# One table of propagation rows, separate tiles, Newton roots on VectorE and the edge copies on ScalarE

## The chip, the cores and the metric

The kernel runs on one core of a Trainium2 chip. The metric is the device time of one execution in microseconds (us). A core has five engines that run side by side, each with its own queue of instructions in order: TensorE (PE; its weight loads are shown as PEld), VectorE (DVE), ScalarE (ACT), GpSimd (POOL) and SyncE (SP). They wait for one another through semaphores. Transfers run on 16 DMA engines; here SyncE issues the plain ones and GpSimd the gathers and scatters by row index.

## The reference

Four graph layers on 50000 nodes with 96 features each and 50000 edges sorted by target:

```python
h = relu(layernorm(x)); x = x + L0(h)    # attention over the edges, 8 heads of 12
h = relu(layernorm(x)); x = x + L1(h)    # message network, segment sum, then
    # update = gelu([h, agg] @ uW1 + ub1) @ uW2 + ub2
    # L1 = layernorm(h + update) * ln_g + ln_b
h = relu(layernorm(x)); x = x + L2(h)    # 16 rounds: h = 0.9 * sum(norm * h[row]) + 0.1 * x, with self loops
h = relu(layernorm(x)); x = x + L3(h)    # graph convolution by edge weight, with W and b
# layernorm(x) = (x - mean) / sqrt(var + 1e-5), without gain and bias
```

L0 needs the edge projection E = edge_attr_96 @ We + be for each edge.

## The kernel before

All tables have 96 columns of f32. 128 partitions hold 392 rows each (ROWS = 50176), and work goes in 49 batches (NB) of 8 columns (J), that is 1024 rows a batch. A node that no edge points to has a static row, whose values depend on itself alone; the rows that edges point to live in SLOTS = 128 x 400 further rows. `row_e` holds for each edge the row to gather: below ROWS it is a static one, above it a slot.

The stages follow one another, with a barrier between: graph tables; the projections of all nodes; **the first dense pass** (lines 722 to 949); the attention pass over the edges; the message pass over the edges (the second edge pass); the first propagation round with the dense work of the last layer beside it; 14 middle rounds; the last round; the last convolution.

The first dense pass does two independent things for each batch. For the edges: TensorE turns the edge features (`turn`, L824), ScalarE copies them to SBUF (`turned`, L869), TensorE multiplies by We (`edge_product`, L841), VectorE copies the result out of PSUM (`evict`, L904), SyncE stores it. For the nodes: the update of L1 as if no message came in. TensorE makes the hidden layer (`hidden`, L832), ScalarE its gelu (L876), TensorE the outer layer (L851), VectorE adds h (`add`, L913), takes mean and variance (`stats`: L331, L336), ScalarE the square root (`ln_root`, L341), VectorE the reciprocal and -mean times it (`scale`: L346, L347), ScalarE normalises (`norm`, 8 activations, L354), VectorE multiplies by the gain, adds the bias and the old x (`update`: L931, L932, L936). Then the same again for the layer norm of x2: `stats2`, a root, `scale2`, and `norm2` with relu. The results x2 and y are the two halves of one tile `yx`. SyncE stores x2 once and y twice, into each of the two tables of propagation rows (`y_t[0]`, `y_t[1]`), since the rounds read one and write the other. GpSimd meanwhile scatters the segment pointers into `kv_t`, 8 scatters a batch (L806). Square root and gelu need different tables of ScalarE, and a load (ACT_TABLE_LOAD) stands before the first use of either after the other. The names in the profile leave digits out: `d_` is the tiles of the dense passes.

Each engine's order is written out by hand as a list of (lag, step) pairs given to `skewed`: in tick t the engine does each step in the order of the list, for batch t - lag. Halves of a batch (4 of 8 columns) are g = 0 and 1. In the first dense pass:

```python
skewed(pe, (1, turn(0)), (4, edge_product(1)), (3, outer_layer(0)), (1, turn(1)), (0, hidden(1)),
       (1, hidden(0)), (1, edge_product(0)), (2, outer_layer(1)))
skewed(act, (0, turned(0)), (4, root2), (3, norm), (0, gelu(0)), (-3, slots), (4, norm2), (-1, gelu(1)),
       (2, root), (0, turned(1)))     # root, root2: the two calls of ln_root
skewed(dve, (3, scale), (3, evict(1)), (2, add(0)), (4, scale2), (2, stats), (3, update),
       (0, evict(0)), (1, add(1)), (3, stats2))
```

`Own` lets an engine wait for its own last instruction: `do` issues one and waits for its end before the next. Tiles have four buffers (K = 4, index h) where DMAs are involved, PSUM tiles one for each half.

Of the kernel before, what the change touches and what calls it, by code (L numbers as in the profile page):

```python
# [36 lines left out]
TURN = 8 * P  # L37
assert NB % 2 == 1 and 0 < TAIL < CH
# [6 lines left out]
EPS = 1e-5  # L45

# [104 lines left out]
def program(nc, x, src, dst, edge_attr_32, edge_attr_96, edge_weight,  # L151
# [21 lines left out]
    y_t = [dram(f"y{k}_t", ROWS + SLOTS, D) for k in range(2)]  # L173
# [7 lines left out]
    with outer:  # L181
# [87 lines left out]
        ptr_e = sb("ptr_e", [P, CH])  # L269
# [452 lines left out]
        with ExitStack() as p0:  # L722
# [26 lines left out]
            s_sl, s_one, s_mv, s_sd, s_rn, s_ln, s_x2, s_mv2, s_sd2, s_rn2, s_y0 = map(sem, (  # L749
                "d1_slots", "d1_ones", "d1_stats", "d1_root", "d1_scale", "d1_ln_ready", "d1_x2_ready", "d1_stats2",  # L750
                "d1_root2", "d1_scale2", "d1_y0_ready"))
            s_own1, s_own2, s_own3, s_own4, s_own5 = map(sem, (
                "d1_vector_stats", "d1_vector_scale", "d1_vector_x2", "d1_vector_stats2", "d1_vector_scale2"))

            with nc.Block() as block:
                @block.sync
                def _(sp):
# [28 lines left out]
                    def store(b, n, h):  # L786
                        after(sp, s_y0, b + 1)
                        sp.sem_inc(s_turn_s)
                        sp.dma_start(rows_of(x2n_t, 0, b), yx[:, h, :, D:2 * D]).then_inc(s_st[h], 16)
                        for t in y_t:  # L790
                            sp.dma_start(rows_of(t, 0, b), yx[:, h, :, 0:D]).then_inc(s_st[h], 16)
                    skewed(sp, (6, store_e), (2, load_x), (-2, load), (7, store), (0, load_h0), (-2, load_turned))
                    clear_stale(sp)
                    for h in range(K):
                        sp.wait_ge(s_se[h], 16 * OF[h])
                        sp.wait_ge(s_st[h], 48 * OF[h])
# [62 lines left out]
                def _(act):  # L859
# [32 lines left out]

                @block.vector
                def _(dve):
                    own1, own2, own3, own4, own5 = (Own(dve, s_own1, 1), Own(dve, s_own2, 1), Own(dve, s_own3, 2),
                                                    Own(dve, s_own4, 1), Own(dve, s_own5, 1))
                    V.memset(eaT[D:D + 1], 1.0).then_inc(s_one, 1)
                    V.memset(uT[D:D + 1], 1.0).then_inc(s_one, 1)

                    def evict(g):  # L900
                        def run(b, n, h):
                            dve.wait_ge(s_se[h], 16 * n)
                            after(dve, s_eo[g], b + 1)
                            V.tensor_copy(ee[:, h, 4 * g:4 * g + 4, :], eo[g][:]).then_inc(s_ee[g], 1)  # L904
                        return run
# [1505 lines left out]
```

## Time and profile before

| | us |
|---|---|
| median of 3 runs | 11803.59 (11793.79 to 11810.04) |
| the profiled execution, its span | 11805.1 |
| first dense pass, about | 560 to 1190 of the span |
| attention pass | 1190 to 1860 |
| message pass | 1860 to 2590 |
| first round and last dense work | 2590 to 3160 |
| 14 middle rounds | 3160 to 10185 |
| last round | 10185 to 10740 |
| last convolution | 10740 to 11805 |

The profiled execution's own time is its span, from the first instruction to the last. Over it TensorE is busy for 58%, VectorE 54%, ScalarE 36% and GpSimd 72%. In the rows below a time like 814.62 is the start in us from the span's start, and the number behind it the length of the piece; x8 says that 8 instructions are merged into it; [3.97 <-ACT d_eaT L869] says that the engine sat idle for 3.97 us before it, and what ended that. Busy time does not count the waits, so an engine can be at 80% and yet no wait-free path run through it.

### The profile page before, as it was taken

The page shows a single profiled execution, that of the slowest core. Times are in us where ns is not written, and L with a number is a line of the kernel's source. Part 1 is how long each engine was busy: PE and PEld are TensorE (multiplying, and loading weights), DVE is VectorE, ACT ScalarE, POOL GpSimd, SP SyncE. Part 2 cuts the span into 40 slices and gives each one's busy share as a digit, 9 for nine tenths or more (in the row PEclk, how much of TensorE's full clock was granted, in tenths as well). Part 3 has the DMA queues.
Part 4 walks back from the last instruction along what each step waited for, and adds up shares of the span by engine and source line. Part 5 has one row for each costly group of instructions (what it writes and reads, how often), then busy time and mean ns, then how long its engine had stood idle before and what let it go on. Part 6 is the DMA issues. An engine that isn't in the chain of part 4 may idle for free. (4 is left out here: it accounts for less than half of the span.)

```text
span 11805.1 us, 140168 instructions
## 1 busy us (share of the span) xinstructions
PE 6807.1 (58%) x20914; PEld 4246.3 (36%) x20914; DVE 6395.0 (54%) x24157; ACT 4285.7 (36%) x14616; POOL 8514.7 (72%) x8690
## 2 busy tenths in 40 slices
PE   4688677966665665655555555655555555672000
PEld 4566566654433332333333323323333333352000
DVE  6577897889744444444444444444444444575443
ACT  5699666978622222222222222222222222373000
POOL 6675765747677777777777777777777777776777
PEclk7666667977777777778777777777777777896555
DMA  7998885668754444444444444444444444573222
GB/s 250 303 252 242 274 275 172 216 217 284 229 157 126 118 113 116 117 113 119 113 115 117 113 119 113 115 117 113 119 113 117 115 113 118 150 233 125 65 67 55
DMA packets 970285, 1804.49 MB, mean 153 GB/s; under 512 B 412879, under 2 KB 423549, under 8 KB 970062
## 3 DMA queue, kind: packets, MB, share of 16 engines
q1 hardware_dynamic: 687725, 1384.14, 34.7%
q0 software_dynamic: 282336, 418.19, 17.0%
q14 instruction: 184, 1.50, 0.0%
q8 instruction: 40, 0.66, 0.0%
HBM read 1070.12 MB, written 738.89 MB: 153 GB/s over the span
## 5 line engine op out<-in xcount | busy, mean ns | idle before, releaser
L365 POOL DMA_INDIRECT r_g<-y_t,idx_s x5768 | 5535.4, 960 | 1947.2 <-issue 1841.0
L1945 DVE SCALAR_TENSOR_TENSOR F<-r_g,scan_s,F 128x96 f32<-128x96 f32 x5488 | 1769.1, 322 | 3974.2 <-DMA r_g<-y_t,idx_s 3147.3
L2074 ACT ACTIVATE H<-r_pu,kc_e 128x96 f32 (+1 forms) x5474 | 1340.2, 355 | 5536.1 <-PE r_pu L2046 5502.2
L2046 PE MATMUL r_pu<-r_S,ident 128*128 128x384 f32 x2688 | 1734.3, 793 | 2797.4 <-DVE r_S L1947 2797.4
L2046 PEld LDWEIGHTS r_pu<-r_S,ident 128*128 128x128 f32 x2688 | 679.4, 278 | 3546.9 <-DVE r_S L1947 3212.0
L1947 DVE SCALAR_TENSOR_TENSOR r_S<-r_S,scan_s,r_g 128x96 f32<-128x96 f32 x5488 | 1719.0, 313 | 0.5
L2028 PE MATMUL r_pu<-H,ident 128*128 (+2 forms) x2744 | 1530.1, 649 | 91.4 <-DMA r_c<-c_t 85.5
L2029 PE MATMUL r_pu<-r_c,ident 128*128 128x384 f32 (+1 forms) x2744 | 1349.0, 579 | 0.0
L2028 PEld LDWEIGHTS r_pu<-H,ident 128*128 128x128 f32 x2744 | 778.1, 284 | 765.1 <-issue 654.6
L2029 PEld LDWEIGHTS r_pu<-r_c,ident 128*128 128x128 f32 x2744 | 666.8, 243 | 559.9 <-issue 361.4
L2335 PE MATMUL e_pc<-e_S,B 128*128 128x96 f32 x2 | 0.7, 474 | 1042.5 <-DVE e_o L2379 1042.5
L365 POOL DMA_INDIRECT e_kv<-kv_t,idx_s x392 | 422.2, 1077 | 244.2 <-issue 126.0
L806 POOL DMA_INDIRECT kv_t<-seg_s,idx_s x392 | 404.1, 1031 | 189.5 <-issue 114.3
L2324 POOL DMA_INDIRECT out<-e_o,e_out_s x393 | 432.2, 1100 | 119.7 <-issue 119.7
L365 POOL DMA_INDIRECT e_g<-z_t,idx_s x392 | 388.7, 992 | 166.0 <-issue 119.2
L365 POOL DMA_INDIRECT e_x<-h_t,idx_s x392 | 379.4, 968 | 134.5 <-issue 107.5
L365 POOL DMA_INDIRECT l_g<-y_t,idx_s x392 | 378.2, 965 | 130.8 <-issue 117.6
L365 POOL DMA_INDIRECT n_x<-in_x,idx_s x392 | 370.2, 944 | 139.8 <-issue 117.5
L2335 PEld LDWEIGHTS e_pc<-e_S,B 128*128 128x128 f32 x2 | 0.5, 310 | 1042.7 <-DVE e_o L2379 1042.7
L2369 DVE TENSOR_TENSOR e_g<-e_g,scan_s 128x768 f32<-128x768 f32 x49 | 47.9, 977 | 553.8 <-DMA e_g<-z_t,idx_s 553.8
L649 PE MATMUL n_kb<-w_kvq,n_hT 97*128 97x192 f32 x784 | 241.6, 494 | 126.0 <-ACT n_hT L682 67.8
L673 ACT ACTIVATE n_h<-n_x,n_rn 128x96 f32<-128x96 f32 x784 | 286.0, 458 | 0.5 <-DVE n_rn L347 0.5
(329 smaller groups left out, 11912.6 us busy)
## 6 DMA issues: line engine op xcount, KB each, us to landing
r_c<-c_t SPq DMA_DIRECT2D x686, 384.0 KB
y_t<-H SPq DMA_DIRECT2D x672, 384.0 KB
r_g<-y_t,idx_s POOLq DMA_INDIRECT x5880
kv_t<-n_kv SPq DMA_DIRECT2D x49, 776.0 KB, 6.9
y_t<-d_yx SPq DMA_DIRECT2D x98, 384.0 KB
agg_t<-e_S SPq DMA_DIRECT2D x49, 416.0 KB, 4.6
x1s_t<-e_xb SPq DMA_DIRECT2D x50, 384.0 KB, 4.8
h_t<-e_h SPq DMA_DIRECT2D x50, 384.0 KB, 5.2
```

The costliest lines, as they stand in the source:

```text
L365: G.indirect_dma_start(out=to(j), out_offset=None, in_=table, in_offset=bass.IndirectOffsetOnAxis(ap=idx_s[:, h, j:j + 1], axis=0)).then_i ...
L649: last = T.matmul(kb[i][:, j % 2, :], hT[:, h, j // 4, j % 4 * P:(j % 4 + 1) * P], w_kvq[:, 0:2 * D], start=True, stop=True)
L673: last = A.activation(hh[:, h, s, j, :], xs[:, h, s, j, :], ACT.Relu, scale=rn[:, h, 0, c], bias=rn[:, h, 1, c])
L806: G.indirect_dma_start(out=kv_t.rearrange("r (a w) -> (r a) w", w=WP), out_offset=bass.IndirectOffsetOnAxis(ap=idx_s[:, h, j:j + 1], axis= ...
L1945: own.add(V.scalar_tensor_tensor(out=F[:, 0:D], in0=g[:, j, :], scalar=scan_s[:, h, j, 1:2], in1=F[:, 0:D], op0=ALU.mult, op1=ALU.add))
L1947: last = V.scalar_tensor_tensor(out=S[:, h % 2, j, :], in0=before, scalar=scan_s[:, h, j, 0:1], in1=g[:, j, :], op0=ALU.mult, op1=ALU.add)
L2028: T.matmul(to, ident[:], cols(H, b)[:, c, :], start=True, stop=False)
L2029: T.matmul(to, ident[:], cs[:, h, c, :], start=False, stop=False)
L2046: last = T.matmul(pu[h % 2][g][:], ident[:], S[:, h % 2, 4 * g:4 * g + 4, :], start=False, stop=True)
L2074: last = A.activation(v[:, j, :], pu[h % 2][j // 4][:, j % 4, :], ACT.Copy, scale=k[:, j, 0:1])
L2324: G.indirect_dma_start(out=out, out_offset=bass.IndirectOffsetOnAxis(ap=dst_s[:, h, j:j + 1], axis=0), in_=ot[:, h, j, :], in_offset=None, ...
L2369: own.do(V.tensor_tensor(g_[:, h], g_[:, h], scan_s[:, h, :, 2:3].to_broadcast([P, J, D]), ALU.mult))
```

## The change

Part 1, tables and tiles. The two tables of propagation rows become one: slots of one kind of round, the static rows, slots of the other kind. The static rows are stored once. Two lists of rows (`row_y`) take the place of `row_e` for the gathers from it; they are computed in seven VectorE operations at the start of the message pass, into two tiles that are free by then. The tile `yx` becomes two tiles `x2` and `y0`.

Part 2, roots. The first dense pass has no activation with Sqrt any more. VectorE makes 1 / sqrt(var + eps) itself: a start value by a shift and a subtraction on the bits, and three Newton steps, 13 operations with those for eps and -mean times it. One call serves both layer norms, on 128x16 numbers: the first norm of batch b and the second of batch b - 1. It stands where `scale` stood; `scale2` goes. VectorE has one tick more.

Part 3, edge projection. `evict` moves from VectorE to ScalarE: evict(1) stands where root2 was, evict(0) where root was. The lags stay.

```diff
+Y_STATIC = SLOTS
+Y_SLOTS = [SLOTS + ROWS, 0]
+Y_ROWS = [ROWS + 2 * SLOTS, SLOTS + ROWS]
...
-    y_t = [dram(f"y{k}_t", ROWS + SLOTS, D) for k in range(2)]
+    y_t = dram("y_t", ROWS + 2 * SLOTS, D)
...
-        ptr_e = sb("ptr_e", [P, CH])
+        ptr_e = sb("ptr_e", [P, CH], I32)
+        row_y = [ptr_e, src_i]
...
+        def root_reciprocals(own, mv, rn):
+
+            y, nb, v, u = (rn[:, k] for k in range(4))
+            own.do(V.tensor_scalar(v, mv[:, :, :, 1], EPS, None, ALU.add))
+            own.do(V.tensor_scalar(u.bitcast(I32), v.bitcast(I32), 1, None, ALU.logical_shift_right))
+            own.do(V.tensor_scalar(y.bitcast(I32), u.bitcast(I32), -1.0, float(ROOT_START), ALU.mult, ALU.add))
+            for _ in range(3):
+                own.do(V.scalar_tensor_tensor(out=u, in0=y, scalar=-0.5, in1=y, op0=ALU.mult, op1=ALU.mult))
+                own.do(V.tensor_tensor(u, u, v, ALU.mult))
+                own.do(V.scalar_tensor_tensor(out=y, in0=u, scalar=1.5, in1=y, op0=ALU.add, op1=ALU.mult))
+            return V.scalar_tensor_tensor(out=nb, in0=mv[:, :, :, 0], scalar=-1.0, in1=y, op0=ALU.mult, op1=ALU.mult)
...
-            yx = sb("d1_yx", [P, K, J, 2 * D], F32, p0)
+            y0 = sb("d1_y0", [P, K, J, D], F32, p0)
+            x2 = sb("d1_x2", [P, K, J, D], F32, p0)
             st = sb("d1_st", [P, 2, J, 6], F32, p0)
-            mv = sb("d1_mv", [P, K, J, 2], F32, p0)
-            rn = sb("d1_rn", [P, K, 3, J], F32, p0)
-            mv2 = sb("d1_mv2", [P, K, J, 2], F32, p0)
-            rn2 = sb("d1_rn2", [P, K, 3, J], F32, p0)
+            mv = sb("d1_mv", [P, K, 2, J, 2], F32, p0)
+            rn = sb("d1_rn", [P, K, 4, 2, J], F32, p0)
...
-                        sp.dma_start(rows_of(x2n_t, 0, b), yx[:, h, :, D:2 * D]).then_inc(s_st[h], 16)
-                        for t in y_t:
-                            sp.dma_start(rows_of(t, 0, b), yx[:, h, :, 0:D]).then_inc(s_st[h], 16)
+                        sp.dma_start(rows_of(x2n_t, 0, b), x2[:, h]).then_inc(s_st[h], 16)
+                        sp.dma_start(rows_of(y_t, Y_STATIC, b), y0[:, h]).then_inc(s_st[h], 16)
...
+                    def evict(g):
+                        def run(b, n, h):
+                            act.wait_ge(s_se[h], 16 * n)
+                            after(act, s_eo[g], b + 1)
+                            A.copy(ee[:, h, 4 * g:4 * g + 4, :], eo[g][:]).then_inc(s_ee[g], 1)
+                        return run
+
                     def norm(b, n, h):
                         after(act, s_x2, b - 3)
-                        ln_norm(act, b, hs[:, h], ln[:, h], rn[:, h], s_rn, ACT.Identity).then_inc(s_ln, 1)
+                        after(act, s_rn, b + 1)
+                        for j in range(J):
+                            last = A.activation(ln[:, h, j, :], hs[:, h, j, :], ACT.Identity,
+                                                scale=rn[:, h, 0, 0, j:j + 1], bias=rn[:, h, 1, 0, j:j + 1])
+                        last.then_inc(s_ln, 1)
 
                     def norm2(b, n, h):
-                        act.wait_ge(s_st[h], 48 * n)
-                        ln_norm(act, b, yx[:, h, :, D:2 * D], yx[:, h, :, 0:D], rn2[:, h], s_rn2, ACT.Relu
-                                ).then_inc(s_y0, 1)
-                    skewed(act, (0, turned(0)),
-                           (4, lambda b, n, h: ln_root(act, b, mv2[:, h], rn2[:, h], s_mv2, s_sd2)),
-                           (3, norm), (0, gelu(0)), (-3, slots), (4, norm2), (-1, gelu(1)),
-                           (2, lambda b, n, h: ln_root(act, b, mv[:, h], rn[:, h], s_mv, s_sd)), (0, turned(1)))
+                        act.wait_ge(s_st[h], 32 * n)
+                        after(act, s_rn, b + 2)
+                        k = (h + 1) % K
+                        for j in range(J):
+                            last = A.activation(y0[:, h, j, :], x2[:, h, j, :], ACT.Relu,
+                                                scale=rn[:, k, 0, 1, j:j + 1], bias=rn[:, k, 1, 1, j:j + 1])
+                        last.then_inc(s_y0, 1)
+                    skewed(act, (0, turned(0)), (3, evict(1)), (3, norm), (0, gelu(0)), (-3, slots), (4, norm2),
+                           (-1, gelu(1)), (0, evict(0)), (0, turned(1)))
...
-                    own1, own2, own3, own4, own5 = (Own(dve, s_own1, 1), Own(dve, s_own2, 1), Own(dve, s_own3, 2),
-                                                    Own(dve, s_own4, 1), Own(dve, s_own5, 1))
+                    own1, own2, own3, own4 = (Own(dve, s_own1, 1), Own(dve, s_own2, 12), Own(dve, s_own3, 2),
+                                              Own(dve, s_own4, 1))
+                    own2.do(V.memset(mv[:], 1.0))
+                    own2.loop()
...
-                    def evict(g):
-                        def run(b, n, h):
-                            dve.wait_ge(s_se[h], 16 * n)
-                            after(dve, s_eo[g], b + 1)
-                            V.tensor_copy(ee[:, h, 4 * g:4 * g + 4, :], eo[g][:]).then_inc(s_ee[g], 1)
-                        return run
...
-                        ln_stats(dve, own1, b, hs[:, h], st[:, 0], mv[:, h], s_mv)
+                        ln_stats(dve, own1, b, hs[:, h], st[:, 0], mv[:, h, 0], s_mv)
 
                     def scale(b, n, h):
                         after(dve, s_ln, b - 3)
+                        after(dve, s_y0, b - 4)
                         own2.step(b)
-                        ln_scale(dve, own2, b, mv[:, h], rn[:, h], s_sd, s_rn)
+                        if not (isinstance(b, int) and b == NB):
+                            after(dve, s_mv, b + 1)
+                        after(dve, s_mv2, b)
+                        last = root_reciprocals(own2, mv[:, h], rn[:, h])
+                        own2.end()
+                        last.then_inc(s_rn, 1)
 
                     def update(b, n, h):
                         own3.step(b)
@@ -932,21 +961,16 @@
                         own3.do(V.tensor_tensor(ln[:, h], ln[:, h], r_all[:, 1:2, :].to_broadcast([P, J, D]), ALU.add))
                         own3.end()
                         dve.wait_ge(s_x[h], 48 * (n + 1))
-                        dve.wait_ge(s_st[h], 48 * n)
-                        V.tensor_tensor(yx[:, h, :, D:2 * D], xs[:, h], ln[:, h], ALU.add).then_inc(s_x2, 1)
+                        dve.wait_ge(s_st[h], 32 * n)
+                        V.tensor_tensor(x2[:, h], xs[:, h], ln[:, h], ALU.add).then_inc(s_x2, 1)
 
                     def stats2(b, n, h):
                         after(dve, s_x2, b + 1)
-                        after(dve, s_rn2, b - 3)
+                        after(dve, s_rn, b - 2)
                         after(dve, s_mv2, b)
-                        ln_stats(dve, own4, b, yx[:, h, :, D:2 * D], st[:, 1], mv2[:, h], s_mv2)
-
-                    def scale2(b, n, h):
-                        after(dve, s_y0, b - 3)
-                        own5.step(b)
-                        ln_scale(dve, own5, b, mv2[:, h], rn2[:, h], s_sd2, s_rn2)
-                    skewed(dve, (3, scale), (3, evict(1)), (2, add(0)), (4, scale2), (2, stats), (3, update),
-                           (0, evict(0)), (1, add(1)), (3, stats2))
+                        ln_stats(dve, own4, b, x2[:, h], st[:, 1], mv[:, (h + 1) % K, 1], s_mv2)
+                    skewed(dve, (3, scale), (2, edges_only(add(0))), (2, edges_only(stats)), (3, edges_only(update)),
+                           (1, edges_only(add(1))), (3, edges_only(stats2)), total=NX)
...
+                    row_f, at_y = seg[:, :, 0], seg[:, :, 1]
+                    first.do(V.tensor_copy(row_f, row_e[:]))
+                    first.add(V.tensor_scalar(at_y, row_f, float(SLOTS), None, ALU.add))
+                    first.do(V.tensor_scalar(row_f, row_f, float(ROWS), None, ALU.is_lt))
+                    first.add(V.tensor_copy(row_y[0][:], at_y))
+                    first.do(V.tensor_scalar(row_f, row_f, float(SLOTS + ROWS), float(-SLOTS - ROWS), ALU.mult,
+                                             ALU.add))
+                    first.do(V.tensor_tensor(at_y, at_y, row_f, ALU.add))
+                    first.do(V.tensor_copy(row_y[1][:], at_y))
...
-                        gathers(y_t[1], lambda j: g_[:, h, j, :], h, s_g[h])
+                        gathers(y_t[0:Y_ROWS[1], :], lambda j: g_[:, h, j, :], h, s_g[h])
...
-                        to = y_t[1 - odd]
+                        to = Y_SLOTS[1 - odd]
...
-                                gathers(y_t[odd], lambda j: g_[:, h % GB, j, :], h, s_g[h])
+                                gathers(y_t[0:Y_ROWS[odd], :], lambda j: g_[:, h % GB, j, :], h, s_g[h])
...
-                            A.copy(idx_s[:, h, :], cols(row_e, b)).then_inc(s_ix, 1)
+                            A.copy(idx_s[:, h, :], cols(row_y[odd], b)).then_inc(s_ix, 1)
```

## Rows read from the trace of the kernel before

**Rows 1.** Stretch, length, busy PE, PEld, DVE, ACT, POOL, PEclk, DMA share, GB/s

```profile
620.00:1100.00 480.00, 408.53 (x1718) 314.86 (x1717) 367.12 (x1679) 437.52 (x1017) 342.31 (x334) 0.61 0.92 257
...
3160.00:10185.00 7025.00, 4141.72 (x8339) 2147.45 (x8340) 3044.88 (x11029) 1477.46 (x6852) 5230.24 (x5488) 0.78 0.43 118
```

**Rows 2.** Line 932: count, min/median/max ns, first and last start in us

```profile
L932 DVE TENSOR_TENSOR d_ln<-d_ln,r_all x49: 957/958/1007, 598.1 to 1178.3; 128x768 f32<-128x768 f32 x49
```

**Rows 3.** Timeline, 811 to 825 us: ScalarE and TensorE

```profile
811.72 0.67 ACT L876 ACTIVATE d_uT<-d_pu,c_u 96x512 f32<-96x512 f32 x1
...
812.41 1.28 ACT L341 ACT_TABLE_LOAD   x1
...
814.62 1.06 PE L824 MATMUL d_te<-ident,d_ea 128*96 128x128 f32 x4 [3.97 <-ACT d_eaT L869]
...
815.06 2.96 ACT L354 ACTIVATE d_ln<-d_h,d_rn 128x96 f32<-128x96 f32 x8
...
815.47 3.62 PE L832 MATMUL d_pu<-d_hT,w_ua 96*96 96x512 f32 x4
...
819.17 1.28 ACT L876 ACT_TABLE_LOAD   x1 [1.15 <-PE d_pu L832]
...
820.47 0.68 ACT L876 ACTIVATE d_uT<-d_pu,c_u 96x512 f32<-96x512 f32 x1
...
824.12 0.67 ACT L876 ACTIVATE d_uT<-d_pu,c_u 96x512 f32<-96x512 f32 x1
```

**Rows 4.** The same timeline: VectorE

```profile
814.11 0.20 DVE L346 RECIPROCAL d_rn<-d_rn 128x8 f32<-128x8 f32 x1 [2.19 <-ACT d_rn L341]
814.35 0.17 DVE L347 SCALAR_TENSOR_TENSOR d_rn<-d_mv,d_rn 128x8 f32<-128x8 f32 x1
814.43 0.55 DVE L904 COPY d_e<-d_eo 128x384 f32<-128x384 f32 x1
...
815.36 0.20 DVE L346 RECIPROCAL d_rn<-d_rn 128x8 f32<-128x8 f32 x1
...
815.77 1.38 DVE L331 BATCH_NORM_STATS2 d_st<-d_h 128x6 f32<-128x96 f32 x8
...
817.30 0.64 DVE L336 BATCH_NORM_AGGREGATE d_mv<-d_st 128x2 f32<-128x6 f32 x8 [0.16 <-DVE d_st L331]
...
818.05 0.96 DVE L931 TENSOR_TENSOR d_ln<-d_ln,r_all 128x768 f32<-128x768 f32 x1
...
820.91 0.55 DVE L904 COPY d_e<-d_eo 128x384 f32<-128x384 f32 x1
```

**Rows 5.** Groups by line, 1230 to 2590 us: busy us, mean ns, idle before

```profile
L1163 ACT COPY e_u<-e_ub 128x384 f32<-128x384 f32 (+1 forms) x99 | 46.4, 470 | 0.2 <-PE e_ub L1102 0.2
```

**Rows 6.** Lines 346, 347 as rows 2; timeline of VectorE at 18 us

```profile
L346 DVE RECIPROCAL n_rn<-n_rn x49: 252/253/254, 56.7 to 542.7; 128x16 f32<-128x16 f32 x49
...
L347 DVE SCALAR_TENSOR_TENSOR n_rn<-n_mv,n_rn x49: 174/176/245, 57.0 to 543.0; 128x16 f32<-128x16 f32 x49
...
18.09 0.15 DVE L518 SCALAR_TENSOR_TENSOR dg<-seen,carry 128x1 f32<-128x1 f32 x1
```

**Rows 7.** Timeline, 1182 to 1184 us: the last norm of the stage

```profile
1182.90 0.20 DVE L346 RECIPROCAL d_rn<-d_rn 128x8 f32<-128x8 f32 x1 [0.44 <-ACT d_rn L341]
1183.13 0.17 DVE L347 SCALAR_TENSOR_TENSOR d_rn<-d_mv,d_rn 128x8 f32<-128x8 f32 x1
...
1183.40 2.97 ACT L354 ACTIVATE d_yx<-d_yx,d_rn 128x96 f32<-128x96 f32 x8 [0.60 <-DVE d_rn L347]
```

**Rows 8.** Timeline of TensorE, 1121 to 1134 us, at the lower clock

```profile
1121.82 1.06 PE L824 MATMUL d_te<-ident,d_ea 128*96 128x128 f32 x4 [3.96 <-ACT d_eaT L869]
...
1131.96 1.92 PE L851 MATMUL d_po<-w_u,d_uT 97*128 97x96 f32 x8
```

**Rows 9.** Groups by line and shape, 700 to 1060 us: the scatters

```profile
L806 POOL DMA_INDIRECT kv_t<-seg_s,idx_s x248 | 254.5, 1026 | 106.3 <-issue 72.5 <-ACT seg_s L863 33.8
```

**Rows 10.** Timeline of VectorE at the start of the message pass

```profile
1888.10 0.56 DVE L1555 SCALAR_TENSOR_TENSOR e_g<-e_gate,e_po 128x384 f32<-128x384 f32 x1 [21.12 <-ACT e_gate L1505]
```

More of the change, by code:

```diff
@@ L45 @@
 EPS = 1e-5
+ROOT_START = 0x5F3759DF
 class Own:
@@ L748, in program @@
                 "d1_po_full", "d1_h_ready"))
[L749 to L753, printed above, removed]
+            s_sl, s_one, s_mv, s_rn, s_ln, s_x2, s_mv2, s_y0 = map(sem, (
+                "d1_slots", "d1_ones", "d1_stats", "d1_scale", "d1_ln_ready", "d1_x2_ready", "d1_stats2",
+                "d1_y0_ready"))
+            s_own1, s_own2, s_own3, s_own4 = map(sem, (
+                "d1_vector_stats", "d1_vector_scale", "d1_vector_x2", "d1_vector_stats2"))
             with nc.Block() as block:
@@ L795, in _ @@
                         sp.wait_ge(s_se[h], 16 * OF[h])
-                        sp.wait_ge(s_st[h], 48 * OF[h])
+                        sp.wait_ge(s_st[h], 32 * OF[h])
                 @block.gpsimd
@@ L1717, in load @@
                         sp.dma_start(xn[:, h], rows_of(x2n_t, 0, b)).then_inc(s_xn[h], 16)
-                        sp.dma_start(yn[:, h], rows_of(y_t[0], 0, b)).then_inc(s_xn[h], 16)
+                        sp.dma_start(yn[:, h], rows_of(y_t, Y_STATIC, b)).then_inc(s_xn[h], 16)
                     def load_own(b, n, h):
@@ L1722, in load_own @@
                         sp.sem_inc(s_turn_s)
-                        sp.dma_start(yo[:, h], slots_of(y_t[1], ROWS, b)).then_inc(s_yo[h], 16)
+                        sp.dma_start(yo[:, h], slots_of(y_t, Y_SLOTS[1], b)).then_inc(s_yo[h], 16)
                     def store_c(b, n, h):
@@ L1732, in store_y @@
                         sp.sem_inc(s_turn_s)
-                        sp.dma_start(slots_of(y_t[0], ROWS, b), ys[:, h]).then_inc(s_st[h], 16)
+                        sp.dma_start(slots_of(y_t, Y_SLOTS[0], b), ys[:, h]).then_inc(s_st[h], 16)
                     def store_z(b, n, h):
@@ L1752, in _ @@
                     sp.wait_ge(s_zv, 1)
-                    sp.dma_start(first_slots(y_t[0], ROWS), zs[:]).then_inc(s_zo, 16)
+                    sp.dma_start(first_slots(y_t, Y_SLOTS[0]), zs[:]).then_inc(s_zo, 16)
                     sp.wait_ge(s_zo, 32)
@@ L1809, in slots @@
                     def slots(b, n, h):
-                        gather_rows(act, n, h, row_e, b, s_ix, s_g)
+                        gather_rows(act, n, h, row_y[1], b, s_ix, s_g)
                         after(act, s_ss, b - 3)
@@ L1975, in store @@
                                 sp.sem_inc(s_turn_s)
-                                sp.dma_start(slots_of(to, ROWS, b)[:, J - 1, :], cols(H, b)[:, J - 1, :]
+                                sp.dma_start(slots_of(y_t, to, b)[:, J - 1, :], cols(H, b)[:, J - 1, :]
                                              ).then_inc(s_st, 16)
@@ L1980, in store @@
                             sp.sem_inc(s_turn_s)
-                            sp.dma_start(slots_of(to, ROWS, b), cols(H, b)).then_inc(s_st, 16)
+                            sp.dma_start(slots_of(y_t, to, b), cols(H, b)).then_inc(s_st, 16)
                         after(sp, s_up, r * NB)
@@ L1985, in one @@
                         after(sp, s_z, r + 1)
-                        sp.dma_start(first_slots(to, ROWS), zs[:]).then_inc(s_zo, 16)
+                        sp.dma_start(first_slots(y_t, to), zs[:]).then_inc(s_zo, 16)
                     rounds(sp, one)
@@ L2008, in step @@
                                 done = s_g[h] if j < J - 2 else s_end[j - J + 2]
-                                G.indirect_dma_start(out=g_[:, h % GB, j, :], out_offset=None, in_=y_t[odd],
+                                G.indirect_dma_start(out=g_[:, h % GB, j, :], out_offset=None, in_=y_t[0:Y_ROWS[odd], :],
                                                      in_offset=bass.IndirectOffsetOnAxis(ap=idx_s[:, h, j:j + 1], axis=0)
@@ L2143, in load @@
                         after(sp, s_up, b - 3)
-                        sp.dma_start(yo[:, h], slots_of(y_t[0], ROWS, b)).then_inc(s_ld[h], 16)
+                        sp.dma_start(yo[:, h], slots_of(y_t, Y_SLOTS[0], b)).then_inc(s_ld[h], 16)
                         sp.dma_start(cs[:, h], slots_of(c_t, 0, b)).then_inc(s_ld[h], 16)
@@ L2168, in step @@
                         after(pool, s_ss, b - 3)
-                        gathers(y_t[0], lambda j: g_[:, h, j, :], h, s_g[h])
+                        gathers(y_t[0:Y_ROWS[0], :], lambda j: g_[:, h, j, :], h, s_g[h])
                     skewed(pool, (0, step))
@@ L2213, in slots @@
                         s_g.wait(act, h, 16 * J * n)
-                        A.copy(idx_s[:, h, :], cols(row_e, b)).then_inc(s_ix, 1)
+                        A.copy(idx_s[:, h, :], cols(row_y[0], b)).then_inc(s_ix, 1)
                         after(act, s_ss, b - 3)
```

8 lines of the change are left out of this document (4 added, 4 removed).

## The prediction

> **What bounds the kernel now.** I read the table of stretches first. The change alters only one stage's arithmetic, the first dense pass (560 to 1190 us of the span); in it no engine is full: TensorE 409 of 480 us, ScalarE 438, VectorE 367, GpSimd 342, at a granted clock of 0.61 [rows 1]. So a loop of waits sets its pace. 49 batches pass; the second multiply of the residual update starts at 598.1 in the first and at 1178.3 in the last, 12.09 us apart on the mean, 580.2 us in all [rows 2]. In the middle the distance is 12.40: that from gelu(1) at 811.72 to the next at 824.12 [rows 3].
>
> The timeline shows the loop. ScalarE: gelu(1) at 811.72, a table load at 812.41, a root, then the copies of the turned edge features; TensorE, idle until the copy, turns at 814.62 and makes both hidden products from 815.47 on, 3.62 us at the lower level of the clock; ScalarE loads the other table only then, at 819.17, does gelu(0) at 820.47, 8 relu norms, and gelu(1) at 824.12 [rows 3]. Both table loads (1.28 us, 1.30 from start to next start) stand in this loop of 12.40. VectorE is not in it: it waits for ScalarE's root until 814.11, and starts the update at 818.05, when the norms (815.06 + 2.96 = 818.02) end [rows 3, 4].
>
> **The change, part by part.**
>
> *Roots and tables.* Sqrt goes, so gelu's set stays loaded: two loads and a root leave the loop. Its new length: 12.40 - 2 x 1.30 - 0.2 for the root's step, plus one copy of an edge half before turned(1), 0.47 by the copy of this shape in the next stage [rows 5] = 10.1 us. ScalarE's own work was 438 / 480 of 12.4 = 11.3 us a batch [rows 1]; less 2.57 for tables and 0.6 for roots, plus 2 x 0.47, it is 9.1. ScalarE stops being the bound; what is late next is VectorE.
>
> The Trainium skill, "ScalarE: Activation LUTs", section "What ACT_TABLE_LOAD costs", adds a drain of about 1.38 us to each load of 1.28. Here gelu ends at 811.72 + 0.67, the load starts 0.02 later [rows 3], and there is no room for one. By the page the loop would lose 5.3 us and not 2.6; the sum would be the same, as VectorE takes over before either.
>
> *VectorE's work.* It loses both evictions (0.47 each from start to next start: one and an add of the same size stand from 814.43 to 815.36), the separate scale steps (814.11 to 814.43, 815.36 to 815.77) and its waits for roots. It gains one chain of 13 operations on 128x16 elements, each waiting for the one before. Their forms are not in the trace. The nearest row is the multiply of 128x16 in the first stage, 0.176 us; the gap to a dependent operation is 0.04 (814.11 + 0.20 to 814.35) [rows 4, 6]. So 12 x 0.216 + 0.18 = 2.77 us. Bounds: the smallest operation, 0.15 + 0.04 a step, gives 2.43; the reciprocal of 128x16, 0.253 + 0.04 a step, gives 3.77 [rows 6]. I take the multiply, since 10 of the 13 are multiplies of that size and none divides.
>
> *VectorE's pace.* The queue is in order: chain(b), add(0), stats, update(b), add(1), stats2. The update needs ScalarE's norm, which needs the chain just done. Before, the norm had an eviction, an add and another scale step besides stats beside it. Now:
> - chain 2.77;
> - to the norm 0.10 (1183.13 + 0.17 to 1183.40), norm 2.96, back 0.03: 3.09 [rows 3, 7]. Beside it lie add(0) 0.46 and stats 1.53 + 0.64 = 2.63 [rows 4], so VectorE waits about 0.45;
> - update 2.86 (818.05 to 820.91), add 0.46, stats2 1.53 + 0.64 + 0.04 = 2.21 [rows 4].
>
> Sum 11.39 us a batch. The last three batches have no add(0), 10.93. 45 x 11.39 + 3 x 10.93 = 545.3 against 580.2: 34.9 us less. After the last stats2 the chain takes 2.77 where a root, reciprocal and multiply took about 0.9 (1182.90 - 0.44 of waiting, to 1183.13 + 0.17): 1.9 more [rows 7]. Net 33 us.
>
> *Edge copies on ScalarE.* Priced above. Evict(1) stands between turned(0) and the norm, so it could delay the norm; ScalarE has 11.39 - 9.1 = 2.3 us of slack a batch, waits there for the chain, and TensorE made that product earlier in its order. Cost 0; if ScalarE were late by all of it, 0.47 x 48 = 23 us. The store of the edge half comes later in the order by some us than before, with four buffers behind it: nothing waits.
>
> *TensorE.* Nothing added. Its whole pass at the lower level is 1131.96 - 1121.82 = 10.14, plus 1.92 less the overlap of 0.21 seen at 814.62 to 815.47 = 11.85 us [rows 3, 8]. That is over 11.39. A granted clock of 0.61 on the mean says that it stands at the lower level (0.5) for about four fifths of the time; in the rest it gets ahead, and then idles, 3.97 us before 814.62 [rows 1, 3]. At the lower level it would fall behind by 0.46 us a batch. There is room for about 1 us: from the chain's start, add(1) is due at 2.77 + 3.09 + 2.86 = 8.7, and from turn(1) to the end of the product that it needs it takes some 7.7 (all of the pass but a turn and two products: 11.85 less 0.85, 1.66 and 1.66). Two batches fit. I take 0, by the wait of 3.96 us at 1121.82 as at 814.62 [rows 8]; if the clock never rises, 11.85 is the pace.
>
> *GpSimd.* Eight scatters a batch, each 1.026 + 0.30 of issue [rows 9]: 10.6 us. Below 11.39, so hidden; it becomes the floor if VectorE's steps are all short.
>
> *DMA and SyncE.* One of the two stores of the propagation rows goes, of eight transfers of one size. The 16 DMA engines are busy for 0.92 now [rows 1]; 7/8 of it in 11.39 and not 12.4 us is 0.88. Also, the separate tiles are contiguous in a partition where the pair alternated every 96 numbers; I give that nothing. Neither was what a wait ended on. Both SyncE issue steps are shorter; it waits for TensorE anyway. Gain 0, or 0.1 us a batch if landings of x or h0 come late today, which no row shows; lower bound 0.
>
> *New tables of rows.* Seven VectorE operations on 392 columns are added at the start of the second edge pass. VectorE idles 21.12 us there before its first work [rows 10]; at 1 us each they lie within. A memset ahead of the first dense pass lies beside loads. In the other stages the same bytes are moved from other addresses. The propagation rounds, 7025 of the 11805 us, are paced by GpSimd (5230 us busy, 5488 gathers, and issue) [rows 1]. A gather is issued from a list of rows, and its length has no term of which tensor it is. I take 0. From both sides: 0.003 us a gather either way is 16 us.
>
> Sum: 11805.1, the span of the profiled execution, less 33 = 11772. That execution is 1.5 us above the median of 11803.6, so 11771.
>
> **The rivals.**
>
> *TensorE paces (18%).* For: 11.85 over 11.39, and 0.61 is much low time. Against: with less idling it should be high at least as often. 45 x 11.85 + 3 x 10.93 = 566.0, net 12 less: 11792.
>
> *Short steps (12%).* The chain is 2.43: the pace 11.05, 49 us less: 11755. For: some are single-source operations. Against: each waits for the one before. The scatters' 10.6 are the end of this road.
>
> *Slower: the chain is long (9%).* In VectorE's queue, ahead of the norm, it stands wholly in the loop. At 3.77 a chain the pace is 12.39, the stage 593 and the tail 2.9: 16 us more, 11820. From 0.26 us a step (chain 3.44) on, nothing is left of the gain. For: 13 waits on its own semaphore, each with a register operation ahead; integer operations that no row shows. Against: the dependent pair at 814.11 has such a wait, too, and costs 0.04.
>
> *Tables are not rid of (4%).* If identity were not in gelu's set, ScalarE would switch twice a batch, two loads in the loop as today, and save only the root's step and the store: about 11800. The trace shows relu after gelu without a load; identity only after the root. The Trainium skill, "ScalarE: Activation LUTs", section "Table sets: the hidden batching unit", has identity in every set; no row here shows it behind gelu.
>
> *The rounds shift (7%).* Stores and gathers of a round share one tensor and other banks of memory. At 0.003 us longer a gather, 16 us more than forecast, 11787; at 0.008, slower than before, 11815. For: 60% of the time lies there. Against: paced by issue.
>
> **How the numbers follow.** The forecast (50%) is 11771, its own range 11760 to 11784. About 24 us (0.2%) is what a measurement can tell from no change: faster is below 11780. Faster: nearly all of the forecast (47), short steps (12) = 59%. Same: TensorE (18), tables (4), the forecast's rest (3), half of the rounds (3) = 28%. Slower: the long chain (9), the other rounds (4) = 13%. The range, 11748 to 11802, takes in the short chain's 11755 and TensorE's 11792, and leaves out the long chain and the worst rounds.
>
> **What would show it.** Right: one table load in the stage; updates 11.3 to 11.5 us apart; 13 small operations of 2.6 to 2.9 us in all; VectorE waiting 0.3 to 0.6 us for the norm in each batch; ScalarE waiting for the chain and no more for the hidden product; the DMA share below 0.88 in the stage; the rounds the same to 3 us each. Wrong: updates 11.8 or more apart with TensorE busy and low throughout; a chain over 3.4 us; table loads at each norm; GpSimd with no idle time, which would mean a pace of 10.6; or stages other than this one moving by over 10 us.

## The result, and the profile after

The forecast was 11771 us. Measured: 11818.5 us median of 20 runs (11808.6 to 11830.0) against 11802.1 for the kernel before (20 runs, 11789.3 to 11812.6); the ratio is 1.0016, 95% interval 1.0009 to 1.0022. The change makes the kernel slightly slower where I forecast 0.3% faster, and the time lies above my range. Of the experiments below, e5 to e8 and e13 to e16 ran at 14.3 ms, the kernel before beside them too (14328.9 and 14314.4 us), so no time of theirs is laid beside the others; what is used of them is the counts of instructions and packets and the waits on issue.

The profiled execution has a span of 11827.8 us. The rows of after that answer to [rows 1], the first dense pass and the propagation rounds (length, busy PE, PEld, DVE, ACT, POOL, clock, DMA share, GB/s):

```profile
620.00:1100.00 480.00, 419.08 (x1819) 326.74 (x1818) 419.06 (x2053) 366.67 (x992) 373.39 (x349) 0.63 0.79 236
3173.00:10197.00 7024.00, 4131.01 (x8344) 2139.77 (x8344) 3044.83 (x11033) 1479.05 (x6860) 5230.05 (x5488) 0.78 0.43 118
```

In the dense pass ScalarE and VectorE have changed places: 438 to 367 us busy and 367 to 419. The rounds are as before. The multiply of the update, which answers to [rows 2], and the table load with the edge copy (busy us, mean ns, idle before):

```profile
L961 DVE TENSOR_TENSOR d_ln<-d_ln,r_all x49: 957/959/961, 596.5 to 1155.6; 128x768 f32<-128x768 f32 x49
```

```profile
L899 ACT COPY d_e<-d_eo 128x384 f32<-128x384 f32 x98 | 46.2, 472 | 0.0
...
L891 ACT ACT_TABLE_LOAD x1 | 1.3, 1283 | 0.0
```

48 distances in 559.1 us, 11.65 each (12.09 before). Of the table loads one is left. The first issue for the next stage, on SyncE's load of its rows, came at 1193.4 us before and at 1170.1 now: 23.3 us gained.

The gain is given back two stages later. The first issues of each stage, us of the span, read from the tile that each stage loads first:

| first issue of | before | after | stage, after less before |
|---|---|---|---|
| attention pass | 1193.4 | 1170.1 | first dense pass and all ahead −23.3 |
| message pass (ScalarE's first copy of a turned tile) | 1873.7 | 1852.5 | attention pass +2.1 |
| first round | 2602.2 | 2613.4 | **message pass +32.4** |
| 14 middle rounds | 3160.6 | 3172.9 | first round +1.1 |
| last round | 10191.8 | 10202.0 | middle rounds −2.1 |
| last convolution | 10735.9 | 10747.6 | last round +1.5 |
| end | 11805.1 | 11827.8 | last convolution +11.0 |

The message pass computes what it computed before. VectorE's waits there, 1850 to 2600 us of after (what waits, for what: us in total, times, longest):

```profile
DVE e_g L1588 <- ACT e_gate L1529: 34.3, 5, 17.8
DVE e_g L1588 <- issue: 33.1, 7, 4.8
```

The second row is new; no such row stands in the same answer for before. "Issue" is time in which the engine waited for nothing that the profile shows, and L1588, the first operation of the loop over four batches, has it seven times, once behind each of the seven jumps back to the loop's start. The timeline shows the place:

```profile
2184.50 1.02 DVE L1588 SCALAR_TENSOR_TENSOR e_g<-e_gate,e_po 128x384 f32<-128x384 f32 x2 [4.82 <-issue]
```

What comes with it is in the table of DMA queues (packets, MB, share; queue 14 brings instructions). For 1850 to 2600 us before, then after, then for 2178 to 2184 us of after, the time of this one wait:

```profile
q14 instruction: 28, 0.23, 0.1%
```

```profile
q14 instruction: 59, 0.48, 0.2%
```

```profile
q14 instruction: 2, 0.02, 1.2%
```

31 more packets of 8 KB, 4.4 for each of 7 jumps; over the whole run 184 became 219. By the packets' own times two or three of them start within 6 us of each jump back in after, and none in e1 or e4 below. So at every jump VectorE's queue fetches its own loop again, and the first operation waits for it.

### The profile page after: what moved, and what is told of

Its sections match the earlier page's. It is cut to its first block and busy times, and to the rows that moved or that the text cites. A ratio compares the mean times of both kernels' runs of the same rounds, so it can differ in the third digit from the quotient of the medians.

```text
span 11827.8 us, 140857 instructions
## 1 busy us (share of the span) xinstructions
PE 6797.3 (57%) x20914; PEld 4251.9 (36%) x20914; DVE 6437.1 (54%) x24521; ACT 4178.3 (35%) x14523; POOL 8534.7 (72%) x8690
## 3 DMA queue, kind: packets, MB, share of 16 engines
q14 instruction: 219, 1.79, 0.0%
```

## The experiments

**Theory.** Instructions come in blocks of one packet, 8 KB. The queue can keep the message pass's loop, 327 VectorE instructions a pass (counted in the records between two branches, the same in both kernels), only if it lies in few enough blocks. The change put 138 instructions ahead of it: 131 in the first dense pass (311 and not 242 in a pass of its loop, and 62 more in the batches written out around it) and the seven table operations. **Rival.** What the change does in the message pass, its table operations and the new rows, costs the 32 us.

**e1 to e4: only the place is moved.** One-column VectorE fills into a tile of their own, put once ahead of the loop where VectorE has no work (here e1; the number is 30 in e2 and e3 and 100 in e4):

```diff
                     first.do(V.memset(S[:, K - 1, J - 1, :], 0.0))
+                    for i in range(90):
+                        V.memset(pad[:, i:i + 1], 0.0)
```

> The changed kernel with 90 one-column VectorE fills added once, ahead of the loop of the message pass (the second edge pass); they fall into the 21 us in which VectorE has no work there. Theory (position of the loop): the change added 138 VectorE instructions ahead of this loop, and in that position its 327 instructions have to be fetched again in every pass of the loop, one stall of about 4.8 us in each of 7 passes. 90 instructions more move it by less than one block of 128 and out of that position: no idle time of over 2 us with the releaser issue ahead of L1590, the pass shorter by 30 to 33 us, the whole 11785 to 11792 us. Rival 1 (the cost comes from what the change does in this pass: its table operations, or the new rows being read): the stalls stay, 11818 to 11824. Rival 2 (more instructions ahead of the loop, whatever their number, make it later): worse than after by some us.

> The kernel before with 30 such fills at the same place and nothing of the change. Theory (position): 30 instructions move the loop from the last place in a block of 128 in which it fits to one in which it doesn't: 7 stalls of 4.5 to 5 us ahead of the loop's first operation, and 11832 to 11838 us against 11803. Rival (what the change does in this pass): no stall, 11802 to 11806 us.

> The changed kernel with 30 fills and not 90. Theory (position, period of 128): 10 + 30 = 40 instructions beyond the place of the kernel before is still in the part of the block where the loop doesn't fit: the 7 stalls stay, 11815 to 11825 us. If any shift cures it, they are gone.

> The kernel before with 100 fills. Theory (position, period of 128): 100 beyond the place before is a place like that of the changed kernel with 90 fills: no stalls, 11800 to 11810 us, though more instructions stand ahead of the loop than with 30. Rival (the number of instructions ahead counts, and not their place): stalls as with 30 or worse.

Measured: e1 11785.4 us (ratio to before 0.9982, 0.9973 to 0.9991); e2 11849.6 (1.0034, 1.0021 to 1.0048); e3 one run, 11838.3; e4 one run, 11795.6; the kernel before beside them 11809.9. The waits on issue and the instruction packets, 1850 to 2600 us, of e1 (no stall, so only the packets stand here), then of e2 and e3:

```profile
q14 instruction: 26, 0.21, 0.1%
```

```profile
DVE e_g L1558 <- issue: 30.0, 7, 4.4
```

```profile
q14 instruction: 59, 0.48, 0.2%
```

```profile
DVE e_g L1591 <- issue: 25.8, 7, 3.9
```

```profile
q14 instruction: 60, 0.49, 0.2%
```

e4 has 28 packets there and no such stall. 30 idle fills in the kernel *before*, without any of the change, bring the seven stalls and 40 us (25 to 57 by the interval; the stalls' own 30.0 us lie in it); 90 more instructions in the *changed* kernel take them away, and by the ratios (1.0016 and 0.9982) 40 us with them. The rival has fallen. e2 and e3 came out some 14 us above what I expected; their message passes, 749.6 and 745.3 us, are within what the stalls explain, and the rest is in the rounds (7036.3 and 7050.7 us) and the last convolution (below).

**e5: two Newton steps.** The loop `for _ in range(3)` becomes `range(2)`. That leaves out the last refinement of each root, so the roots are less exact; it is a probe of the chain's place, not the same computation.

> The changed kernel with two Newton steps in place of three (rounds 2 of the root are left out), nothing else. Theory 1 (the chain stands wholly in VectorE's loop of the first dense pass): three operations of 0.21 us less in each of 48 distances, 0.63 x 48 = 30 us: the updates 11.0 us apart, the next stage's first issue near 1140. Rival (another engine is close behind, GpSimd's eight scatters at 10.6 to 11.0 a batch, or TensorE): 11.2 to 11.5 apart, 8 to 20 us. Rival 2 (chain off the loop): 11.6 apart. Theory 2 (position of the loop): 54 VectorE instructions fewer stand ahead of the message pass's loop, 44 before its place in the kernel before, inside a stretch where it fits: no stall of over 2 us with the releaser issue, and the message pass near 716 us, as in e1. Both together: 11750 to 11762 us; with the chain but the stalls kept, 11785 to 11795.

**e6, e7, e8:**

> The new table of propagation rows and its seven VectorE operations, with the first dense pass of the kernel before (one store of its rows fewer), and 90 fills ahead of the message pass's loop to hold it where it fits. Theory (rows at other addresses cost nothing, one store fewer gains nothing): the same stages as the kernel before with 100 fills (e4): dense pass to the next stage 1191 to 1193, message pass 714 to 717, rounds 7031 to 7035, 11792 to 11800 us. Rival 1 (the one table makes the rounds' gathers or the last convolution slower: the changed kernel's profile had 1080 us there against 1069): last convolution 1080 or more and 11805 to 11812. Rival 2 (the store gone gains in the dense pass): its end at 1185 or before.

> The changed kernel with the two copies of the edge projection back on VectorE at their old places in its order, and 30 fills ahead of the message pass's loop. Theory (VectorE's queue paces the dense pass): two copies of 0.47 us come into its loop, less the 0.36 us in which it waits for the norm anyway: 0.58 to 0.94 a batch, 28 to 45 us; updates 12.2 to 12.6 apart, next stage near 1200, so that nothing of the change's gain is left; 11813 to 11830 us against the changed kernel without stalls (e1, 11785). Rival (ScalarE or TensorE paces): 11.6 to 11.8 apart, 11785 to 11795.

> The changed kernel with 118 fills: the loop of the message pass stands 128 instructions beyond its place in the kernel before. Theory (blocks of 128): the same place within a block as in the kernel before: no stalls with the releaser issue, 25 instruction packets in the message pass and not 58. Rival (e1 and e4 hit a stretch by chance, no period of 128): stalls of 3 to 5 us may stand there.

The ratios of e5, e6 and e7 to the kernel before beside them were 1.0058, 0.9998 and 0.9990, and e8 is one run; what is used is the packets. e8 has 185 in the whole run (184 before): the place repeats after 128, as expected. e6 and e7 have 184. e5 has 229, and not where I had looked: its message pass has 24, but its *first dense pass* has these, and the waits at that loop's first two operations (600 to 1580 us):

```profile
q14 instruction: 60, 0.49, 0.2%
```

```profile
DVE d_rn L358 <- issue: 50.3, 9, 7.3
...
DVE d_rn L359 <- issue: 29.3, 9, 4.3
```

Stalls at all nine jumps back of a loop that had become shorter; e8 beside it has 0.9 us on issue at L358 and none at L359. This the theory explains only with the count: from the dense loop's start to the message loop's are 1723 instructions in the changed kernel, 13 blocks and 59. Taking all places together (0 is the message loop's place in the kernel before, counted in instructions ahead):

| kernel | place | modulo 128 | refetched |
|---|---|---|---|
| before | 0 | 0 | no |
| after, e12 | 138 | 10 | yes |
| e2 | 30 | 30 | yes |
| e3 | 168 | 40 | yes |
| e5 | 84 | 84 | no |
| e7, e11 | 219 | 91 | no |
| e6, e10 | 97 | 97 | no |
| e4, e13, e17 | 100 | 100 | no |
| e1, e14, e15, e18 | 228 | 100 | no |
| e9, e16 | 114 | 114 | no |
| e8 | 256 | 0 | no |

A loop of 327 touches three blocks of 128 if it starts in the first 58 places of a block, and four otherwise. The column fits if the kernel before stood at one of the places 48 to 57. Then the changed kernel's dense loop stood at one of the first 9 places of a block, and e5's, 15 earlier, across its border: four blocks for 287 instructions. Its second stall fits this too: the border would lie 7 to 15 instructions behind the loop's start, and in the records L359, which waits, is the 11th.

The Trainium skill, "Runtime: NRT & Kernel Launch", section "Instruction fetch mechanics", says that a taken branch whose target is out of the instruction window forces a fetch, an "ifetch stall"; the traces agree. It gives blocks of 256 instructions, two of them held. By that a loop of 327 would be refetched in one stretch of 70 places out of 256; the table has it at 30, 138 and 168 and not at 84 to 114 or 219 to 256, which is no such stretch, and 1.79 MB in 219 packets is 8.2 KB a packet. By these runs the block is 128.

**e9 to e12, with the place taken care of.** e9 is e5 with 30 fills at the start of the first dense pass, where VectorE waits 13 us for its first product. e10 has the new table alone (the dense pass of before, with one store of rows fewer) and 90 fills ahead of the message pass's loop. e11 has 30 there and gives the copies of the edge projection back to VectorE:

```diff
-                    skewed(act, (0, turned(0)), (3, evict(1)), (3, norm), (0, gelu(0)), (-3, slots), (4, norm2),
-                           (-1, gelu(1)), (0, evict(0)), (0, turned(1)))
+                    skewed(act, (0, turned(0)), (3, norm), (0, gelu(0)), (-3, slots), (4, norm2),
+                           (-1, gelu(1)), (0, turned(1)))
...
-                    skewed(dve, (3, scale), (2, edges_only(add(0))), (2, edges_only(stats)), (3, edges_only(update)),
-                           (1, edges_only(add(1))), (3, edges_only(stats2)), total=NX)
+                    skewed(dve, (3, scale), (3, evict(1)), (2, edges_only(add(0))), (2, edges_only(stats)),
+                           (3, edges_only(update)), (0, evict(0)), (1, edges_only(add(1))), (3, edges_only(stats2)), total=NX)
```

> The changed kernel with two Newton steps, and 30 one-column fills at the start of the first dense pass, where VectorE waits for its first product for 13 us. In e5 the dense pass itself fetched instructions in each pass of its loop (53 packets against 14): by the theory of blocks of 128 its loop of 287 stood 15 instructions earlier than the changed kernel's of 311, across the border of a block. Theory 1 (position): 30 later it fits, and the message pass's loop, 14 before its place in the kernel before, fits as well: 184 or 185 packets in the whole run, no stall with the releaser issue in either pass. Theory 2 (the chain stands in VectorE's loop): updates near 11.0 us apart, next stage near 1140; in all 11750 to 11765 us. Rival (GpSimd or TensorE is close behind the chain): 11.2 to 11.5 apart, 11765 to 11780. If the position were not it: 53 packets in the dense pass again.

> The kernel of e6 again, whose chip ran every kernel of that call at 14.3 ms and so cannot be laid beside the others. The expectation is that of e6: theory (rows at other addresses and one store fewer cost and gain nothing) 11792 to 11800 us, dense pass ending 1191 to 1193, rounds 7031 to 7035; rival 1 (the one table slows the rounds or the last convolution by 10 us) 11805 to 11812; rival 2 (the store gone shortens the dense pass) its end at 1185 or before.

> The kernel of e7 again, for the same reason: the changed kernel with the two edge copies back on VectorE, 30 fills ahead of the message pass's loop. Theory (VectorE's queue paces the dense pass): updates 12.2 to 12.6 apart, next stage near 1200, 11813 to 11830 us. Rival (ScalarE or TensorE paces): 11.6 to 11.8 apart, 11785 to 11795. On e6's chip this kernel ended the dense pass at 1533 us and the changed kernel with the copies on ScalarE at 1551, which speaks for the rival.

> The changed kernel itself beside the others of this call. Theory: 11815 to 11825 us, 7 stalls of 4.6 to 4.8 us in the message pass, last convolution between 1069 and 1083 us by chance of the execution. Rival (the last convolution is longer by the change): 1080 again here, and in e9 to e11 all but none under 1075.

| run | median us | ratio to before, 95% | dense pass ends | message pass |
|---|---|---|---|---|
| e9 | 11757.9 | 0.9953 (0.9939 to 0.9966) | 1141.9 | 719.3 |
| e10 | 11812.2 | 1.0001 (0.9992 to 1.0010) | 1190.0 | 720.9 |
| e11 | 11816.4 | 1.0001 (0.9992 to 1.0010) | 1190.8 | 724.9 |
| e12 | 11833.6 | 1.0016 (1.0007 to 1.0025) | 1170.5 | 755.7 |
| before | 11812.7 | | 1193.4 | 728.5 |

(The last two numbers of the kernel before are those of its own profile.) The updates of e9, then of e11:

```profile
L964 DVE TENSOR_TENSOR d_ln<-d_ln,r_all x49: 957/958/1021, 595.1 to 1128.0; 128x768 f32<-128x768 f32 x49
```

```profile
L961 DVE TENSOR_TENSOR d_ln<-d_ln,r_all x49: 957/958/960, 595.1 to 1176.3; 128x768 f32<-128x768 f32 x49
```

e9: 532.9 / 48 = 11.10 a batch, 0.55 below the changed kernel for three steps of 0.21, 0.63 in all: the chain stands in the loop, and no other engine is close enough behind to keep more than 0.08 of it. e9 has 14 instruction packets in the dense pass and 184 in all. It beats both kernels, before by 55 us, of which the first 21 to 28 are the change's own (below) and the rest the step of the root that it leaves out. e11: 581.2 / 48 = 12.11, 0.46 above: two copies are 0.94, and the 0.49 in which VectorE waited for the norm covered the rest. I had expected 0.58 at least, and the end near 1200; it was 1191. With the copies on VectorE nothing of the gain is left, so the new roots gain nothing without their move to ScalarE; the move without the new roots was not run. e10's dense pass ends at 1190: the store that is gone gives at most 3 us, within chance. Its 11812.2 us lie where I had put rival 1, but the kernel before beside it took 11812.7, and its rounds (7036.2 us) are among the others (7029 to 7051). e12 repeats the result with the same seven stalls; its waits on issue add up to 37.6 us in 8, the eighth (3.98 us at the stage's first operation, also in e18) in the place of a wait that elsewhere ends on ScalarE. Without the stalls the message pass took 714.6 to 728.5 us, with them 745.3 to 760.9; the kernel before has the longest of the first kind.

**e13 to e18: the worth of the change, and the last convolution.** e13 and e17 are the kernel of e4, now with enough runs for a ratio; e14 is that of e1; e15 and e18 are e1 with the table of rows made as long as both old ones together, so that all later tensors stand where they stood (`dram("y_t", 2 * ROWS + 2 * SLOTS, D)`); e16 is e9 with that table. The ratios of e13 to e16 were 1.0001, 1.0004, 1.0000 and 1.0025; I conclude nothing from them, nor on what was expected of them.

> The kernel before with 100 fills (e4 again, timed). Theory: both kernels have a place in which the message pass takes 715 us; the kernel before, in its own place, takes 728. So the ratio to before is 0.9986 to 0.9992 (10 to 16 us), and e14 minus this is the worth of the change with the position taken out: 20 to 25 us by the dense pass alone, 10 to 12 if the changed kernel loses some 10 us elsewhere. Rival: e4's 11796 was chance, the ratio is 1.000.

> The changed kernel with 90 fills (e1 again). Theory: 0.9982 again, last convolution between 1069 and 1083 by chance. Rival (the changed kernel's last convolution is longer, by where its tensors stand): 1078 or more.

> The kernel of e14 with the one table of rows made as long as the two of the kernel before together (the added rows are never read or written), so that every later tensor stands where it stood before. Theory of addresses: last convolution 1069 to 1073, and some 8 us less than e14. Theory of chance: the same as e14 within 4 us, whatever the last convolution of its profile.

> The kernel of e9 with the longer table. Theory of addresses: some 8 us less than e9 stood against before: 0.9945. Theory of chance: 0.995 as e9, 11750 to 11765 us.

e17 and e18 are the first and the third of these once more:

> The kernel of e13 again, since e13's chip ran every kernel of that call at 14.3 ms. Theory: ratio to before 0.9986 to 0.9992, message pass 715 us. Rival: 1.000.

> The kernel of e15 again, for the same reason: the changed kernel with 90 fills, the later tensors where they stood before. Theory of addresses: last convolution 1069 to 1073 us and a ratio to before of 0.9975. Theory of chance: 0.9982 as e1.

e17: 11815.9, ratio 1.0004 (0.9995 to 1.0013), message pass 719.7. e18: 11786.1, ratio 0.9980 (0.9971 to 0.9989), last convolution 1073.2. So e4's 11796 was chance; the kernel before lost nothing by its place. With the place taken out the change is worth 0.9982 or 0.9980 against 1, the kernel before in its own place, or against e17's 1.0004: 0.18 to 0.24%, 21 to 28 us. The dense pass is 23 of them. And e18 is no better than e1 beyond the intervals: no cost of the new addresses shows.

The last convolution's 11 us can't be laid to the change. It took 1069.2, 1072.6, 1078.6 and 1082.3 us in the profiles without the change (before, e4, e17, e2) and 1070.8, 1073.2, 1076.6, 1078.7, 1080.2, 1080.5 and 1083.3 in those with it (e9, e18, e11, e12, after, e1, e3; 1078.7 in e10 too). The row that moves is the scatter into the output: 436.8 us busy (1111 ns each) in e4 and 445.6 (1134 ns each) in e17, one kernel in two executions.

## Why the prediction was wrong, point by point

**The step that failed** is the one on the new tables and the other stages: the work there was priced, operation by operation, and "I take 0" for what the stages do; that the change moves every later instruction of VectorE's program was no term and no rival. It costs 32 us by the message pass of before and after, 40 by the ratios of after and e1, 44 by the profiles of these two, and it turns a gain of some 23 us into a loss of 16. The seven operations and the addresses themselves show no cost, as taken (e10, e18), and my last line on what would show it wrong, another stage moving by over 10 us, is what happened.

**The term that was mis-sized** is VectorE's pace: 11.39 forecast, 11.65 measured, 33 us net forecast and 23.3 measured. A batch of after on VectorE, chain, norm's wait, update, statistics:

```profile
847.24 0.17 DVE L358 TENSOR_SCALAR d_rn<-d_mv 128x16 f32<-128x16 f32 x1
...
849.89 0.56 DVE L936 TENSOR_TENSOR d_h<-d_h,d_po 128x384 f32<-128x384 f32 x1
...
853.06 0.96 DVE L960 TENSOR_TENSOR d_ln<-d_ln,r_all 128x768 f32<-128x768 f32 x1 [0.40 <-ACT d_ln L906]
...
855.92 0.55 DVE L936 TENSOR_TENSOR d_h<-d_h,d_po 128x384 f32<-128x384 f32 x1
856.38 1.37 DVE L336 BATCH_NORM_STATS2 d_st<-d_x 128x6 f32<-128x96 f32 x8
...
858.69 0.17 DVE L358 TENSOR_SCALAR d_rn<-d_mv 128x16 f32<-128x16 f32 x1
```

Chain to update 5.82 (forecast 5.86), update 2.86, add 0.46, statistics to the next chain 2.31 (forecast 2.21). That is 11.45. The rest is what VectorE's queue adds in a pass of four batches: 0.22 ahead of the update's last add in two of them, and once 0.31 ahead of the chain, where the loop jumps back and the records have four register operations, some 0.09 us apart, ahead of the chain's first:

```profile
835.56 0.20 DVE L358 TENSOR_SCALAR d_rn<-d_mv 128x16 f32<-128x16 f32 x1 [0.31 <-DVE d_mv L341]
...
838.12 0.21 DVE L365 SCALAR_TENSOR_TENSOR d_rn<-d_mv,d_rn 128x16 f32<-128x16 f32 x1
...
843.60 0.96 DVE L965 TENSOR_TENSOR d_x<-d_x,d_ln 128x768 f32<-128x768 f32 x1 [0.22 <-DVE d_ln L961]
```

0.26 more in 48 distances is 12.5 us. Against it stood the tail, forecast 1.9 us longer and in fact 0.6 shorter (from the last multiply to the next stage's issue 14.5 us, 15.1 before), and a first update 1.6 us earlier.

**What held.** The loop of two table loads was the bound and went with them: one load is left, with identity (L906) and relu (L915) standing between gelus. The chain is 13 operations from 835.56 to 838.33, 2.77 us as forecast (2.72 in the next batch); the nearest row, a multiply of the same size, was the right price for the integer forms as well. VectorE's queue paces the stage (e9, e11), with 0.49 of waiting for the norm a batch where I had 0.45. The copies on ScalarE cost nothing: it waits for the chain 133.5 us in the stage, for the hidden product 12.8, so it has slack. TensorE didn't take over, at a granted clock of 0.63 (from 700 to 1060 us VectorE never waits for it); the DMA share fell from 0.92 to 0.79, below my 0.88. The rounds stayed (7029.1 us, 7031.2 before).

**The rivals.** TensorE's pace, short steps, the long chain, tables that stay and rounds that shift: none came. The long chain's price (11820) came within 2 us of the measured time by luck: its mechanism, a chain of 3.77 us, did not happen.

## What to carry over

Price an edit also by how many instructions it puts ahead of every later loop of the same engine, and look at the instruction queue's packets and at waits on "issue" before a loop's first operation in every stage, also those that the change doesn't touch. Some tens of idle instructions at a place with slack can be worth more than the edit; before an edit is called worthless, run it with such idle instructions ahead of the loops, or two effects of one size will be read as one. Where a chain of small dependent operations stands in the queue ahead of what the other engine needs, each step is paid nearly in full (0.18 of 0.21 us here), so the cheapest gain is one step fewer.

## What the runs showed of the hardware that I had not expected

A VectorE loop of 327 instructions is fetched anew at each jump back, 4 to 5 packets of 8 KB and a stall at its first operation, in places that fit four blocks of 128, and in none that fit three; the stall gets shorter as the loop moves on in its block (33.1 / 7 = 4.7 us at 10 places beyond the kernel before, 30.0 / 7 = 4.3 at 30, 25.8 / 7 = 3.7 at 40).
